# Four of the 64 products by C of each scan run: made by VectorE, not by GpSimd

## The chip, the cores and the metric

The kernel runs on one core of one Trainium2 chip. The metric is the device time of one execution in microseconds (us). The chip's engines each follow a queue of their own: TensorE (PE in the profile, its weight loads PEld), VectorE (DVE), ScalarE (ACT), GpSimd (POOL) and SyncE (SP), which here issues the transfers.

## What is computed

Two sequences of 1024 tokens with 256 features pass through four layers: a linear attention, a state space layer over permuted tokens, a state space layer that runs forward and backward over the tokens, and an attention. The change concerns the state space recurrence of the second and third layers. In the reference (here of the third; the second has the same form):

```python
delta = softplus(einsum('bsr,er->bse', dlt, Wdt) + bdt)
dA = exp(delta[..., None] * A)
dBu = delta[..., None] * Bm[:, :, None, :] * u[..., None]
def step(h, xs):
    dA_t, dBu_t, C_t = xs
    h = dA_t * h + dBu_t
    y = einsum('ben,bn->be', h, C_t)
    return (h, y)
```

There are 512 channels and 16 states for each channel. What the change moves to another engine is part of the product of h by C, inside the `einsum` for y.

## The kernel before

Every engine's program is written out by hand in the order in which it runs, and semaphores join them (`sig`, `wait_ge`, `then_inc`). The recurrence is done in six **runs** (`Run`, q = 0 to 5): two for the second layer, one for each sequence, and four for the third, one for each sequence and direction. Below they are called runs 1 to 6, in the order of their time.

A run is a string of 128 **units**. The sequence of 1024 tokens is cut into two chunks of 512; a unit is one chunk, one of the 16 states and one block (dt) of 128 of the 512 channels. The first chunk's 64 units come first, then the second's. Unit i belongs to step k = i // 4 and to **pair** i // 2, so a run has 64 pairs, each of 128 x 1024 elements, in a ring of five buffers `r.H[pair % HS]` with HS = 5. For unit i:

- ScalarE makes the decay exp(delta A) (`decay`, L931) into one of four buffers. It also scales the operands of u by B (`scale_b`, L908, and `spread_b`, L915) and, in the first chunk, keeps each pair's last column as the start of the second chunk (`keep`, L923, signal `carried`). Its call for pair p stands at i = 2p + 5, behind that unit's decay.
- TensorE forms u = delta x B in one of four PSUM banks (`form_u`, L840 for odd steps, L846 for even ones). It runs three units ahead of the scans, and needs the scan four units back to be done.
- VectorE scans: `tensor_tensor_scan` at L1000, h = a h + u, with a from SBUF and u from PSUM. A new pair's first scan waits until the pair five before it is added up.
- GpSimd multiplies the pair in place by C (`run_p`, L1019), two operands in SBUF. It waits for both scans, in the first chunk for `carried`, and for the row of C, which SyncE loads for each step into one of two buffers (`run_sp`, L801).
- TensorE adds the products up into four PSUM banks (`add_up`, L865); in its order pair p is added at i = 2p + 7. At four places of each chunk it adds a skip product too (`add_skip`, L872).

At unit 71 (`TAKEN_AT`) the first chunk's sum is complete and is taken out of PSUM: by ScalarE (`take_s`, L812) in runs 1, 2, 3 and 5, by VectorE (`take_v`, L818) in runs 4 and 6. After the last unit the second chunk's is taken. In runs 1, 2, 4 and 6 TensorE turns the first chunk's sum back (L1029) between the additions of pairs 62 and 63, and VectorE takes it over with L1036; in runs 3 and 5 TensorE starts the next run's projection (L256) before the additions of pairs 62 and 63.

The lines around the change:

```python
for i in range(UNITS):
    k, dt = divmod(i, 4)
    if i == TAKEN_AT:
        take_y(0)
    w.wait_ge(*decayed.at((q, i)))
    w.wait_ge(*formed.at((q, i)))
    if i >= 2 * HS:
        w.wait_ge(*added.at((q, i // 2 - HS)))
```

Of the kernel before, what the change touches and what calls it, by code (L numbers as in the profile page):

```python
# [8 lines left out]
ALU = mybir.AluOpType  # L9
# [102 lines left out]
def program(nc, T, out):  # L112
    with ExitStack() as ctx:
# [5 lines left out]
        def sig(name, step=1):  # L119
            every.append(Sig(ctx.enter_context(nc.semaphore(name)), step))  # L120
            return every[-1]
# [35 lines left out]
        pe, act, dve, pool = sig("psum_filled"), sig("scalar_done"), sig("vector_done"), sig("pool_done")  # L157
        spread, scaled, formed = sig("b_diagonal"), sig("scaled_by_b"), sig("u_formed")
        decayed, scanned, carried = sig("decayed"), sig("scanned"), sig("carried")
        weighed, added = sig("weighed_by_c"), sig("added_up")  # L160
        taken = sig("y_taken")
        dma = {}

        def transfer(name):
            return dma[name]
# [7 lines left out]
        def area(off, *shape):  # L173
            n = 1
            for s in shape:
                n *= s
            assert off + n <= AW, (off, n)
            v = A[:, off:off + n]
            if len(shape) == 2:
                v = v.rearrange("p (a b) -> p a b", a=shape[0])  # L180
            if len(shape) == 3:
                v = v.rearrange("p (a b c) -> p a b c", a=shape[0], b=shape[1])
            return v
# [429 lines left out]
        CB = [area(WK + 7168 + 512 * j, 512) for j in range(2)]  # L613
        w2all = W2[:, 4992:7040]
        UNITS, PAIRS_N, HS = 128, 64, 5

        class Run:

# [132 lines left out]
        def first_copied(r, j):  # L751
            return (dve if first_state(r, j)[2] else act).at(("dut", r.q, 0, j))
# [31 lines left out]
        def second_half(w, r):  # L784

            w.wait_ge(*act.at(("dut", r.q, 1, 3)))
            w.wait_ge(*dve.at(("dut", r.q, 1, 1)))
# [5 lines left out]
        def run_sp(e, w, r):  # L793
            q = r.q
            w.wait_ge(*transfer(f"c_store{q}").at(0))
            w.wait_ge(*dve.at(("du", q, 0)))
            for k in range(32):
                ci, s = r.steps[k]
                if k >= 2:
                    w.wait_ge(*weighed.at((q, 2 * (k - 2) + 1)))  # L800
                e.dma_start(CB[k % 2], scrc[q][s:s + 1, ci * 512:(ci + 1) * 512].partition_broadcast(128)).then_inc(*transfer(f"c_load{k % 2}").up((q, k)))  # L801

        def took(r, p, j):
# [18 lines left out]
        def run_t(e, w, r, back=None, early=None):  # L822
            q = r.q
            opened = set()

            def form_u(i):
                k, dt = divmod(i, 4)
                if k < 32:
                    ci = r.steps[k][0]
                    if ci == r.order[1]:  # L830
                        second_half(w, r)
                    if i >= 4:
                        w.wait_ge(*scanned.at((q, i - 4)))
                    else:
                        w.wait_ge(*first_copied(r, i))
                    o = PS[:, 4 + i % 4, :]
                    if k % 2:
                        w.wait_ge(*spread.at((q, k, 3)))
                        for j in range(4):
                            t = e.matmul(o[:, j * 128:(j + 1) * 128], r.DUT[:, 4 * ci + j, dt * 128:(dt + 1) * 128], DB[k // 2 % 2][:, j, :],  # L840
                                         start=True, stop=True)
                    else:
                        for j in range(4):
                            w.wait_ge(*(dve.at(("scaled", q, j)) if k == 0 and first_state(r, j)[2] else scaled.at((q, k, j))))
                        for j in range(4):
                            t = e.transpose(o[:, j * 128:(j + 1) * 128], r.G[(2 * k + j) % 6][:, dt * 128:(dt + 1) * 128], ident[:, :])  # L846
                    t.then_inc(*formed.up((q, i)))

            def open_y(ci, j):

                if (ci, j) in opened:
                    return False
                opened.add((ci, j))
                if ci == r.order[0]:
                    w.wait_ge(*(dve if j < 2 else act).at(("dut", q, 1, j)))
                else:
                    w.wait_ge(*took(r, 0, j))
                return True

            def add_up(pair):  # L860
                ci = r.steps[pair // 2][0]
                w.wait_ge(*weighed.at((q, pair)))
                for dt in (pair % 2 * 2, pair % 2 * 2 + 1):
                    for j in range(4):
                        t = e.matmul(PS[:, j, dt * 128:(dt + 1) * 128], r.H[pair % HS][:, dt % 2, j * 128:(j + 1) * 128], ident[:, :],  # L865
                                     start=open_y(ci, j), stop=True, is_transpose=True, skip_group_check=True)
                t.then_inc(*added.up((q, pair)))

            def add_skip(ci, dt):
                w.wait_ge(*dve.at(("diag", q)))  # L870
                for j in range(4):
                    e.matmul(PS[:, j, dt * 128:(dt + 1) * 128], r.U[:, dt, ci * 512 + j * 128:ci * 512 + (j + 1) * 128], diag[:, dt, :],  # L872
                             start=open_y(ci, j), stop=True, skip_group_check=True)

            for i in range(3):
                form_u(i)
            for i in range(UNITS):
                k, dt = divmod(i, 4)
                ci, s = r.steps[k]
                if dt % 2 and i >= 7:  # L880
                    add_up((i - 7) // 2)
                form_u(i + 3)
                if 1 <= i < 5:
                    turn_du_t(e, w, r, 1, i - 1)
                if dt == 3 and 4 <= s < 8:
                    add_skip(ci, s - 4)
            banks.at, banks.held = 4, [[("last y", q, j)] for j in range(4)] + [[("last u", q, j)] for j in range(4)]
            for pair in range(PAIRS_N - 3, PAIRS_N):
                if pair == PAIRS_N - 1 and back:
                    back(0)  # L890
                add_up(pair)
                if pair == PAIRS_N - 3 and early:
                    early()
            if back:
                back(1)
# [78 lines left out]
        def run_v(e, w, r, y, back=None):  # L974
            q = r.q

            def take_y(p):
                for j in range(4):
                    if not by_scalar(r, p, j):
                        take_v(e, w, r, p, j, y)  # L980

            for i in range(UNITS):
                k, dt = divmod(i, 4)
                ci, s = r.steps[k]
                if i == TAKEN_AT:
                    take_y(0)
                if i in (5, 6):
                    copy_du_v(e, w, r, 1, i - 5)
                if i == 6:
                    w.wait_ge(*pe.at(("dut", q, 1, 3)))  # L990
# [4 lines that stand above are left out]
                init = 0.0  # L995
                if ci == r.order[1]:
                    w.wait_ge(*carried.at((q, 2 * s + dt // 2)))
                    init = CAR[:, 4 * s + dt:4 * s + dt + 1]
                h, a, u = (v[:, ::-1] if r.rev else v for v in (r.H[i // 2 % HS][:, dt % 2, :], A_B[i % 4], PS[:, 4 + i % 4, :]))
                e.tensor_tensor_scan(h, a, u, init, ALU.mult, ALU.add).then_inc(*scanned.up((q, i)))  # L1000
            if back:
                back(0)
            take_y(1)
            if back:
                back(1)
            for j in range(4):
                banks.give(("last y", q, j), took(r, 1, j))
                banks.give(("last u", q, j), scanned.at((q, UNITS - 4 + j)))

        def run_p(e, w, r):  # L1010
            q = r.q
            for pair in range(PAIRS_N):
                k = pair // 2
                w.wait_ge(*scanned.at((q, 2 * pair + 1)))
                if r.steps[k][0] == r.order[0]:
                    w.wait_ge(*carried.at((q, pair)))
                w.wait_ge(*transfer(f"c_load{k % 2}").at((q, k)))
                h = r.H[pair % HS]
                e.tensor_tensor(h, h, CB[k % 2].unsqueeze(1).broadcast_to([128, 2, 512]), ALU.mult).then_inc(*weighed.up((q, pair)))  # L1019
# [955 lines left out]
```

## Time and profile before

| | |
|---|---|
| median of three runs | 1950.43 us (1948.98 to 1952.22) |
| span of the profiled execution | 1947.4 us |
| its own time | not given apart from the span |
| VectorE busy | 1602.8 us, 82% of the span |
| TensorE busy | 1845.8 us, 95% |
| ScalarE busy | 1424.0 us, 73% |
| GpSimd busy | 1049.0 us, 54% |
| mean granted clock of TensorE | 0.978 of full speed |

The span goes from the first to the last instruction of the profiled execution. Shares are averages over stages with different limits; the six runs lie between 205 and 1426 us, and what bounds them is read from their own rows. In a timeline neighbouring instructions of one group are merged: the first number is the start, the second the time that they cover, xN their count, and in brackets stands the idle time of the engine before them with what ended it. Recorded durations of VectorE's and GpSimd's instructions overlap a little, so the pace is a little shorter than the duration.

### The profile page before, as it was taken

What the parts mean: (1) busy time and instruction counts of PE and PEld (TensorE: products, weight loads), DVE (VectorE), ACT (ScalarE), POOL (GpSimd) and SP (SyncE); (2) the same over time, 40 slices, a digit from 0 to 9 for tenths busy, and PEclk for the clock granted to TensorE, in tenths of its full rate; (3) what the DMA queues carried; (4) which work ended last, traced back from release to release, by engine and by line L of the source; (5) the groups of instructions that cost most, each with busy time, mean ns of one, the idle gap of its engine ahead of it and who ended that gap; (6) DMA issues with size and microseconds to landing.
All of it is one profiled execution on the core that took longest, in us unless ns stands there. A gap on an engine that the chain in (4) does not pass through costs nothing.

```text
span 1947.4 us, 32682 instructions
## 1 busy us (share of the span) xinstructions
PE 1845.8 (95%) x12312; PEld 1335.2 (69%) x12312; DVE 1602.8 (82%) x2125; ACT 1424.0 (73%) x2661; POOL 1049.0 (54%) x603
## 2 busy tenths in 40 slices
PE   6989899998999999999999999999998999999997
PEld 3664899848998599969995899689974333332323
DVE  5565799678998699989995999889977999999742
ACT  3426899468993899799974999799954377777775
POOL 3031599526994299939980699479944400003000
PEclk9989899998999999999999999999998799999999
DMA  5022111111111112101110111021101111111000
GB/s 202 1 85 99 61 55 61 44 64 33 56 60 37 52 51 60 51 24 55 56 44 2 44 55 56 24 75 57 56 15 33 37 42 37 37 36 36 18 23 22
DMA packets 57547, 95.18 MB, mean 49 GB/s; under 512 B 14951, under 2 KB 23559, under 8 KB 55982
## 3 DMA queue, kind: packets, MB, share of 16 engines
q1 hardware_dynamic: 55854, 88.90, 14.9%
q0 software_dynamic: 1536, 4.20, 0.7%
q8 instruction: 97, 1.59, 0.3%
q14 instruction: 60, 0.49, 0.1%
HBM read 73.55 MB, written 6.91 MB: 41 GB/s over the span
## 4 chain that ended last, share of the span: by engine, by line
PE 66%; POOL 9%; ACT 9%; DVE 8%; issue 6%; DMA 1%; SPq 1%; DVEq 0%; ACTq 0%; POOLq 0%
PE PS L865 12%; PE PS L840 11%; POOL A L1019 8%; PE PS L256 7%; PE PS L1603 6%; PE PS L1556 6%; PE PS L846 5%; PE PS L1763 5%; PE PS L265 3%; DVE A L1569 2%; PE PS L872 2%; ACT A L931 2%; PE PS L441 2%; ACT A L908 1%; DVE ST L206 1%
## 5 line engine op out<-in xcount | busy, mean ns | idle before, releaser
L1019 POOL TENSOR_TENSOR A<-A 128x1024 f32<-128x1024 f32 x384 | 897.7, 2392 | 228.7 <-ACT small L923 104.4
L931 ACT ACTIVATE A<-A,negA 128x512 f32<-128x512 f32 x768 | 546.7, 714 | 30.8 <-DVE A L1000 24.1
L1000 DVE TENSOR_TENSOR_SCAN A<-A,PS 128x512 f32<-128x512 f32 x384 | 435.8, 1200 | 46.6 <-PE PS L846 24.1
L1000 DVE TENSOR_TENSOR_SCAN A<-A,small,PS 128x512 f32<-128x512 f32 x384 | 453.9, 1258 | 8.0 <-ACT A L931 5.0
L865 PE MATMUL PS<-ident,A 128*128 128x128 f32 x3072 | 409.1, 276 | 21.5 <-ACT A L737 13.1
L840 PE MATMUL PS<-A 128*128 128x128 f32 x3072 | 384.2, 276 | 1.5 <-ACT A L915 1.2
L865 PEld LDWEIGHTS PS<-ident,A 128*128 128x128 f32 x3072 | 352.9, 143 | 31.2 <-ACT A L737 15.6
L840 PEld LDWEIGHTS PS<-A 128*128 128x128 f32 x3072 | 363.2, 192 | 4.3 <-DVE A L1000 2.8
L1569 DVE TENSOR_REDUCE A<-PS 128x1 f32<-128x512 f32 x512 | 319.5, 681 | 40.2 <-PE PS L1556 38.7
L1800 ACT ACTIVATE A<-PS 128x512 f32<-128x512 f32 x512 | 267.4, 602 | 102.1 <-PE PS L1763 101.9
L908 ACT ACTIVATE A<-A,small 128x512 f32<-128x512 f32 x320 | 228.3, 714 | 21.7 <-PE PS L846 21.3
L1556 PE MATMUL PS<-A 99*128 99x512 bf16 x480 | 186.9, 398 | 14.0 <-DMA A<-scr 7.5
L846 PE MATMUL PS<-ident,A 128*128 128x128 f32 x1360 | 190.4, 278 | 5.9 <-ACT A L737 2.6
L256 PE MATMUL PS<-A,W 128*128 128x512 f32 (+1 forms) x416 | 184.9, 598 | 3.3 <-DVE A L766 2.9
L1763 PE MATMUL PS<-A 102*128 102x512 bf16 x480 | 178.4, 385 | 5.1 <-ACT A L1800 4.9
L846 PEld LDWEIGHTS PS<-ident,A 128*128 128x128 f32 x1360 | 158.7, 143 | 11.9 <-issue 4.6
L1534 POOL CAST W<-W 128x32 bf16<-128x32 f32 x32 | 6.8, 211 | 291.7 <-DVE W L1527 216.7
L1556 PEld LDWEIGHTS PS<-A 99*128 99x128 bf16 x480 | 47.1, 98 | 167.1 <-DVE A L1569 122.2
L230 POOL TENSOR_TENSOR RS<-VE,HALF 128x8 f32<-128x8 f32 (+1 forms) x15 | 25.7, 1714 | 245.1 <-DVE VE L225 245.1
L915 ACT ACTIVATE A<-ident,small 128x128 f32<-128x128 f32 x384 | 148.8, 394 | 7.3 <-PE PS L840 7.3
L256 PEld LDWEIGHTS PS<-A,W 128*128 128x128 f32 (+1 forms) x416 | 75.1, 185 | 102.7 <-issue 91.5
L1603 PE MATMUL PS<-A,W 128*32 128x512 f32 x1024 | 135.9, 604 | 0.0
(194 smaller groups left out, 1802.5 us busy)
## 6 DMA issues: line engine op xcount, KB each, us to landing
A<-scrc SPq DMA_DIRECT2D x192, 256.0 KB, 3.1
A<-A SPq DMA_DIRECT2D x360, 32.0 KB
scr<-A SPq DMA_DIRECT2D x4, 1024.0 KB, 4.8
W<-in_wa SPq DMA_DIRECT2D x2, 1536.0 KB, 9.7
X<-in_x SPq DMA_DIRECT2D x4, 512.0 KB, 5.5
scr<-W SPq DMA_DIRECT2D x128, 1.5 KB
out<-X SPq DMA_DIRECT2D x4, 512.0 KB, 2.9
W<-in_w SPq DMA_DIRECT2D x1, 1984.0 KB, 7.7
```

What stands on the lines that cost most here:

```text
L256: t = e.matmul(o[0:M, :], wt(k, m), act_in(k), start=k == 0, stop=k == nk - 1)
L840: t = e.matmul(o[:, j * 128:(j + 1) * 128], r.DUT[:, 4 * ci + j, dt * 128:(dt + 1) * 128], DB[k // 2 % 2][:, j, :], start=True, stop=True)
L846: t = e.transpose(o[:, j * 128:(j + 1) * 128], r.G[(2 * k + j) % 6][:, dt * 128:(dt + 1) * 128], ident[:, :])
L865: t = e.matmul(PS[:, j, dt * 128:(dt + 1) * 128], r.H[pair % HS][:, dt % 2, j * 128:(j + 1) * 128], ident[:, :], start=open_y(ci, j), stop ...
L931: e.activation(A_B[i % 4], r.DT[:, dt, ci * 512:(ci + 1) * 512], ACT.Exp, scale=negA[:, r.n, dt * 16 + s:dt * 16 + s + 1]).then_inc(*decay ...
L1000: e.tensor_tensor_scan(h, a, u, init, ALU.mult, ALU.add).then_inc(*scanned.up((q, i)))
L1019: e.tensor_tensor(h, h, CB[k % 2].unsqueeze(1).broadcast_to([128, 2, 512]), ALU.mult).then_inc(*weighed.up((q, pair)))
L1556: e.matmul(o, SQ[j][0:99, nt * 128:(nt + 1) * 128], SK3[j][0:99, c * 512:(c + 1) * 512], start=True, stop=True).then_inc(*pe.up(("trial", ...
L1569: e.tensor_reduce(NM[:, k % 2, q:q + 1], bank(("trial", k, nt, c)), AX.X, ALU.max, negate=True).then_inc(*dve.up(("trial", k, nt, c)))
L1603: t = e.matmul(PV[32 * j:32 * j + 32, c, :], V[:, tile * 272 + 17 * h:tile * 272 + 17 * h + 32], PX[mt % 2][j][:, c * 512:(c + 1) * 512], ...
L1763: e.matmul(o, SK3[sl][0:102, mt * 128:(mt + 1) * 128], SQ[sl][0:102, c * 512:(c + 1) * 512], start=True, stop=True).then_inc(*pe.up(("scor ...
L1800: e.activation(PX[mt % 2][j][:, c * 512:(c + 1) * 512], bank(key), ACT.Exp).then_inc(*act.up(("weights", u, mt, j, c)))
```

## The change

A table `ON_VECTOR` names pairs 15, 31, 47 and 63. GpSimd leaves them out; VectorE multiplies each of them with one `tensor_tensor`, in place, with the same operands. In VectorE's order pair 15's product stands ahead of the scan of unit 34, pair 31's ahead of unit 66, pair 47's ahead of unit 98, and pair 63's behind the last scan. The product has a signal of its own, and TensorE and the loads of C wait for the one or the other; the loads now wait for both pairs of a step.

```diff
+        ON_VECTOR = (15, 31, 47, 63)
+
+        def weighed_at(q, pair):
+            return (weighed_v if pair in ON_VECTOR else weighed).at((q, pair))
...
                 if k >= 2:
-                    w.wait_ge(*weighed.at((q, 2 * (k - 2) + 1)))
+                    w.wait_ge(*weighed_at(q, 2 * (k - 2)))
+                    w.wait_ge(*weighed_at(q, 2 * (k - 2) + 1))
...
-                w.wait_ge(*weighed.at((q, pair)))
+                w.wait_ge(*weighed_at(q, pair))
...
+            def weigh(pair):
+                k = pair // 2
+                w.wait_ge(*scanned.at((q, 2 * pair + 1)))
+                if r.steps[k][0] == r.order[0]:
+                    w.wait_ge(*carried.at((q, pair)))
+                w.wait_ge(*transfer(f"c_load{k % 2}").at((q, k)))
+                h = r.H[pair % HS]
+                e.tensor_tensor(h, h, CB[k % 2].unsqueeze(1).broadcast_to([128, 2, 512]), ALU.mult).then_inc(*weighed_v.up((q, pair)))
+
             for i in range(UNITS):
                 k, dt = divmod(i, 4)
                 ci, s = r.steps[k]
+                if i % 2 == 0 and i // 2 - 2 in ON_VECTOR:
+                    weigh(i // 2 - 2)
...
+            weigh(PAIRS_N - 1)
             if back:
                 back(0)
             take_y(1)
...
             for pair in range(PAIRS_N):
+                if pair in ON_VECTOR:
+                    continue
```

The order of VectorE's instructions in the first run, of the kernel before. L1000 are the scans (with a carried start from unit 64 on, where `small` is an operand), L1036 and L820 what follows the run:

```order
L1000 SCALAR_TENSOR_TENSOR A<-A,PS 128x512 x5
L748 COPY A<-PS 128x512
L1000 SCALAR_TENSOR_TENSOR A<-A,PS 128x512
L748 COPY A<-PS 128x512
L1000 SCALAR_TENSOR_TENSOR A<-A,PS 128x512 x58
L1000 SCALAR_TENSOR_TENSOR A<-A,small,PS 128x512 x64
L1036 TENSOR_TENSOR A<-PS,A 128x512 x4
L820 COPY A<-PS 128x512 x2
L1036 TENSOR_TENSOR A<-PS,A 128x512 x4
```

And of the changed kernel, in which the scans stand at L1016 and the products at L994, from unit 6 on:

```order
L1016 SCALAR_TENSOR_TENSOR A<-A,PS 128x512 x28
L994 TENSOR_TENSOR A<-A 128x1024
L1016 SCALAR_TENSOR_TENSOR A<-A,PS 128x512 x30
L1016 SCALAR_TENSOR_TENSOR A<-A,small,PS 128x512 x2
L994 TENSOR_TENSOR A<-A 128x1024
L1016 SCALAR_TENSOR_TENSOR A<-A,small,PS 128x512 x32
L994 TENSOR_TENSOR A<-A 128x1024
L1016 SCALAR_TENSOR_TENSOR A<-A,small,PS 128x512 x30
L994 TENSOR_TENSOR A<-A 128x1024
L1055 TENSOR_TENSOR A<-PS,A 128x512 x4
```

The four products stand behind units 33, 65, 97 and 127; everything else keeps its place. On GpSimd the 64 products of a run become 60, and nothing takes their place.

## Rows read from the trace of the kernel before

**Rows 1.** Page, costliest groups: busy, mean ns | idle before, by releaser
```profile
L1019 POOL TENSOR_TENSOR A<-A 128x1024 f32<-128x1024 f32 x384 | 897.7, 2392 | 228.7 <-ACT small L923 104.4
L1000 DVE TENSOR_TENSOR_SCAN A<-A,small,PS 128x512 f32<-128x512 f32 x384 | 453.9, 1258 | 8.0 <-ACT A L931 5.0
```

**Rows 2.** Timeline of DVE, first run, from unit 31 on
```profile
248.32 5.85 DVE L1000 TENSOR_TENSOR_SCAN A<-A,PS 128x512 f32<-128x512 f32 x5 [0.58 <-PE PS L840]
254.46 2.33 DVE L1000 TENSOR_TENSOR_SCAN A<-A,PS 128x512 f32<-128x512 f32 x2 [0.29 <-PE PS L840]
257.12 29.20 DVE L1000 TENSOR_TENSOR_SCAN A<-A,PS 128x512 f32<-128x512 f32 x26 [0.33 <-PE PS L840]
286.24 9.46 DVE L1000 TENSOR_TENSOR_SCAN A<-A,small,PS 128x512 f32<-128x512 f32 x8
296.79 27.11 DVE L1000 TENSOR_TENSOR_SCAN A<-A,small,PS 128x512 f32<-128x512 f32 x23 [1.09 <-ACT A L931]
324.14 8.59 DVE L1000 TENSOR_TENSOR_SCAN A<-A,small,PS 128x512 f32<-128x512 f32 x7 [0.24 <-PE PS L840]
332.94 30.57 DVE L1000 TENSOR_TENSOR_SCAN A<-A,small,PS 128x512 f32<-128x512 f32 x26 [0.21 <-PE PS L840]
365.38 2.48 DVE L1036 TENSOR_TENSOR A<-PS,A 128x512 f32<-128x512 f32 x4 [1.88 <-PE PS L1029]
```

**Rows 3.** Timeline of POOL, first run (pairs 12 to 63), then the third run's last 48
```profile
243.60 9.50 POOL L1019 TENSOR_TENSOR A<-A 128x1024 f32<-128x1024 f32 x4 [1.10 <-DVE A L1000]
254.20 111.89 POOL L1019 TENSOR_TENSOR A<-A 128x1024 f32<-128x1024 f32 x48 [1.10 <-DVE A L1000]
...
716.04 111.91 POOL L1019 TENSOR_TENSOR A<-A 128x1024 f32<-128x1024 f32 x48 [1.09 <-DVE A L1000]
```

**Rows 4.** Who waited for L1019, whole span: us, times
```profile
  PE PS L865: 4.9, 5
```

**Rows 5.** Groups of DVE by form: two operands of 2048 elements
```profile
L774 DVE TENSOR_TENSOR A<-A 128x2048 f32<-128x2048 f32 x12 | 27.5, 2292 | 0.4
```

**Rows 6.** Timeline at 1464 to 1470 us: DVE, then POOL
```profile
1464.62 1.22 DVE L1480 TENSOR_TENSOR A<-A 128x1024 f32<-128x1024 f32 x1
...
1467.74 3.15 DVE L1480 TENSOR_TENSOR A<-A 128x1024 f32<-128x1024 f32 x1
...
1467.31 2.50 POOL L1480 TENSOR_TENSOR A<-A 128x1024 f32<-128x1024 f32 x1 [5.32 <-ACT A L1470]
```

**Rows 7.** Timeline at 1498 us: DVE, then POOL
```profile
1498.22 1.89 DVE L1573 TENSOR_TENSOR W<-A 128x8 f32<-128x8 f32 x1
...
1497.96 2.13 POOL L1484 TENSOR_TENSOR A<-A 128x1024 bf16<-128x1024 f32 x1
1500.05 2.13 POOL L1480 TENSOR_TENSOR A<-A 128x1024 f32<-128x1024 f32 x1
```

**Rows 8.** Timeline of ACT at 250 us: the keep of pair 15
```profile
250.40 0.19 ACT L923 ACTIVATE small<-A 128x2 f32<-128x2 f32 x1
```

**Rows 9.** Timelines at 291 to 296 us: PE, then ACT
```profile
291.23 1.95 PE L840 MATMUL PS<-A 128*128 128x128 f32 x16
293.01 1.04 PE L865 MATMUL PS<-ident,A 128*128 128x128 f32 x8
...
294.09 2.06 ACT L812 ACTIVATE A<-PS 128x512 f32<-128x512 f32 x4 [1.97 <-PE PS L865]
```

**Rows 10.** Timeline of DVE, fourth run, at unit 71
```profile
942.98 2.46 DVE L818 TENSOR_TENSOR A<-A,PS 128x512 f32<-128x512 f32 x4
```

**Rows 11.** Timeline of PE, end of the first run and of the third
```profile
363.82 1.09 PE L865 MATMUL PS<-ident,A 128*128 128x128 f32 x8 [0.85 <-POOL A L1019]
364.75 1.91 PE L1029 MATMUL PS<-ident,A 128*128 128x128 f32 x16
366.49 1.04 PE L865 MATMUL PS<-ident,A 128*128 128x128 f32 x8
...
824.65 3.60 PE L256 MATMUL PS<-A,W 128*96 128x512 f32 x8
828.08 1.91 PE L865 MATMUL PS<-ident,A 128*128 128x128 f32 x16
```

More of the change, by code:

```diff
@@ L159, in program @@
         decayed, scanned, carried = sig("decayed"), sig("scanned"), sig("carried")
-        weighed, added = sig("weighed_by_c"), sig("added_up")
+        weighed, weighed_v, added = sig("weighed_by_c"), sig("weighed_by_c_on_vector"), sig("added_up")
         taken = sig("y_taken")
```

## The prediction

> **What bounds the kernel now.** I read the costliest groups first, then the timelines of the runs, one engine at a time, then the waits. On the page GpSimd's products look like the thing to relieve: 384 of them, 2.39 us each, the largest group of all [rows 1]. The timelines say something else. From pair 16 on GpSimd does 48 products back to back in 111.89 us, 2.33 us each [rows 3]. In the same stretch VectorE scans just as densely: 26 units in 29.20 us in the first chunk, 1.12 us each, and 26 in 30.57 us in the second, 1.18 us each [rows 2], or 2.25 and 2.35 us for a pair. So two engines are full at nearly one pace, and the question is which one holds the other.
>
> The brackets of VectorE's rows answer it. From unit 34 to the last scan it idles 0.29 + 0.33 + 1.09 + 0.24 + 0.21 = 2.16 us, and each time for TensorE's forming of u or for ScalarE's decay, never for a sum that waits for GpSimd [rows 2]. GpSimd falls behind a little in the first chunk: its product of pair 32 starts at 254.20 + 16 x 2.33 = 291.5, while the pair's scans end at 286.24 + 2 x 1.18 = 288.6. That lag of 2.9 us is its largest, and it shrinks in the second chunk, where VectorE is the slower one. The ring of five buffers has room: between the end of a pair's scans and the start of the pair five later lie four pairs, 9.0 us, of which the product and the adding (2.37 + 1.04 us) take 3.4, so that 5.6 us are left for a lag. In the whole trace TensorE waits for GpSimd five times, 4.9 us [rows 4], one of them the 0.85 us at the first run's end [rows 11]. VectorE sets the pace of a run, and work taken off GpSimd frees nothing that anyone waits for, while work put on VectorE is put on the path, except where it falls into an idle stretch.
>
> **The price of one product on VectorE.** Two operands in SBUF, 1024 elements: 1.22 us recorded in a row that ran alone [rows 6]. Instructions overlap by some 0.08 us (a scan is recorded with 1.26 us [rows 1] and goes at 1.18 [rows 2]), so it takes 1.14 us of the queue; half of a product of 2048 elements, 2.29 us, is the same [rows 5]. The same group shows the danger: the next instruction of that kind takes 3.15 us [rows 6]. It starts at 1467.74, GpSimd's product runs from 1467.31 to 1469.81, and 1469.81 + 1.14 is 1470.95, near its end at 1470.89: it stood until GpSimd was done. VectorE's scans have one operand in PSUM, and are not stretched by GpSimd; the moved products have both in SBUF. The Trainium skill, SBUF — State Buffer, "Who interferes with whom", says that a VectorE instruction with two SBUF inputs contends with a GpSimd instruction that reads SBUF, and that issue order decides who is blocked for the other's whole length; this speaks against the change, and the trace agrees [rows 6]. By it each moved product would cost from 1.14 us to 1.14 and a whole GpSimd product.
>
> **Part by part, in run 1.** Pair 15, ahead of unit 34. Its `keep` is done at 250.59 [rows 8], before scan 33 ends (248.32 + 3 x 1.16 = 251.8), so that wait costs nothing. GpSimd's pair 14 ends at about 250.7 and pair 16 starts at 254.20 [rows 3], so nothing is in the way: 1.14 us. Right behind it VectorE idled 0.29 and 0.33 us for TensorE [rows 2], which is late there for reasons of its own (the skip products); 0.62 us is covered, 0.52 remains. The row of C was loaded long before.
>
> Pair 31, ahead of unit 66. Scan 65 now ends at 288.6 + 0.5 = 289.1. GpSimd's pair 30 ends at 254.20 + 15 x 2.33 = 289.2, and its next one, pair 32, is released by the same scan 65. I charge 0.15 us of waiting: 1.3 us. That VectorE gets in between two products of GpSimd is shown once: a tiny product of VectorE, issued at 1498.22 beneath GpSimd's instruction, ends at 1500.11, and GpSimd's next takes its usual 2.13 us [rows 7]. VectorE is now 1.8 us late. What follows is the stall for ScalarE at unit 72, 1.09 us [rows 2]. It comes down from TensorE: the forming of units 70 and 71 (from 291.23), the adding of pair 31 (293.01), ScalarE's four copies (294.09), the decay, the scan [rows 9]. TensorE does not wait for GpSimd here (pair 31 was ready at 291.5), so an earlier product gains nothing. It does need scan 67, which ended at 286.24 + 4 x 1.18 = 291.0, and wanted it at about 292.1, so it has 1.15 us of room. Of the 1.8 us about 1.2 vanish there, and 0.6 remain. The stall exists four times, in runs 1, 2, 3 and 5 (ScalarE's 5.0 us over all second chunks [rows 1]); in runs 4 and 6 VectorE takes the sum itself, without idling [rows 10], and all 1.8 us stay. Both pairs: 4 x 0.6 + 2 x 1.8 = 6.0 us over the six runs.
>
> Pair 47, ahead of unit 98. GpSimd, relieved of pair 31, no longer lags, and is between pairs 46 and 48; VectorE's product stands directly behind scan 97 and is there first. 1.14 us, less the 0.21 us of idling before unit 102 [rows 2]. Behind that 26 scans follow without a gap, so 0.93 us stays: 6 x 0.93 = 5.6 us.
>
> Pair 63, behind the last scan. GpSimd's ended at 254.20 + 111.89 = 366.09 [rows 3], 2.6 us after the last scan (332.94 + 30.57 = 363.51); VectorE's would end about 0.1 + 1.14 = 1.3 us after it, sooner by 1.3. But TensorE adds pair 63 only at 366.49, behind the turning of the first chunk's sum, for which it waits on pair 62 [rows 11]. Pair 62 stays on GpSimd. In the third run the adding begins at 828.08 directly behind the next run's projection [rows 11], with GpSimd done at 827.95 [rows 3]: TensorE again. So the 1.3 us is hidden; VectorE idled 1.88 us there anyway [rows 2]. What is gained is GpSimd's small lag at pair 62, about 0.15 us a run: -0.9 us in all.
>
> GpSimd's 24 products fewer, the new waits on TensorE, and SyncE's wait for both pairs of a step cost nothing: pair 15 used to be ready at about 253.1, as it will be now, and GpSimd runs out of work, not of C.
>
> **Sum.** 6.0 + 5.6 - 0.9 = 10.7 us. Against the profiled span, 1947.4 + 10.7 = 1958.1; the median of the three runs lies 3.0 us above that span, so the forecast is 1950.4 + 10.7 = **1961.1 us**, 0.5% slower. No change can be told from one within 0.2%, 3.9 us.
>
> **Rivals.**
> *GpSimd gets in first.* If at pair 31, where both are due within 0.2 us, GpSimd's next product goes ahead in every run, VectorE stands for 2.33 us more: 6 x 2.33 = 14 us, 1975. How such a block looks stands in [rows 6]; [rows 7] speak against it.
>
> *No cover.* If TensorE and ScalarE are late along with VectorE, none of the idling absorbs anything: three products in six runs, 18 x 1.14 = 20.5 us, 1971. For it: TensorE is dense too, and forms u only after the scan four back. Against it: TensorE's room of 1.15 us. Both together are given one chance.
>
> *Nearly all is hidden.* If TensorE was late at unit 72 by more than I read, so that runs 1, 2, 3 and 5 keep nothing of pairs 15 and 31, and the last product's 1.25 us does count in every run: 2 x 1.8 + 5.6 - 7.5 = +1.7 us, 1952. Against it speak the two ends of runs in [rows 11].
>
> *GpSimd is the pacemaker.* If the ring of five buffers held the scans to GpSimd's pace, each of three products would take 2.33 us off its string and put 1.14 on VectorE, and the end would come 1.25 us sooner: 3 x 1.19 + 1.25 = 4.8 us a run, 29 us, 1921 us. It decides from a lag of some 5.6 us on, and the trace shows 2.9; and VectorE has only 2.16 us of idling to give up from unit 34 on against 3.4 us of new work.
>
> **Chances and range.** My forecast, with sums from 1956 to 1966: 0.58. Slower still by a lost port or no cover: 0.28. Nearly hidden: 0.10. GpSimd the pacemaker: 0.04. The range reaches from 1955, where runs 1, 2, 3 and 5 hide both early products, to 1973, above the case without cover and below the one in which every port is lost. Slower 0.86, within 0.2% 0.10, faster 0.04.
>
> **What would show it.** VectorE should have 24 products with a mean near 1.25 us; one of 3 us or more is a lost port. ScalarE's 5.0 us before the second chunks' scans should be nearly gone, and so the 0.29 and 0.33 us before units 36 and 38. From the first scan to the last, run 1 should be about 1.5 us longer, run 4 some 2.7. The waiting of TensorE for GpSimd should stay about what it is, and the stretch from the last scan to L1036's turn should grow by nothing. I am wrong if the runs become shorter, if the scans' own duration changes, or if VectorE's idling grows by itself behind the products.

## The result and the profile after

The changed kernel takes 1960.91 us (median of four runs, 1957.24 to 1961.37) against 1951.24 us of the kernel before: a ratio of 1.0045, with a 95% interval of 1.0033 to 1.0058. (A ratio given here or below can differ by up to 0.1% from that of the two medians.) It is slower, as forecast, and 1961.1 was close. The trace shows that the sum was nearer than its terms: the number is partly right by luck, since errors of both signs cancel, and one of the rivals that I thought less likely turned out to be a real mechanism.

The page of the changed kernel, its costliest groups for the scans, the products left on GpSimd and ScalarE's decay, columns as in [rows 1]:

```profile
span 1959.0 us, 32684 instructions
...
L1038 POOL TENSOR_TENSOR A<-A 128x1024 f32<-128x1024 f32 x360 | 849.6, 2391 | 270.9 <-DVE A L1016 110.0
L936 ACT ACTIVATE A<-A,negA 128x512 f32<-128x512 f32 x768 | 547.8, 716 | 43.2 <-DVE A L1016 34.0
...
L1016 DVE TENSOR_TENSOR_SCAN A<-A,small,PS 128x512 f32<-128x512 f32 x384 | 454.0, 1255 | 2.9 <-PE PS L845 2.2
```

The span grew from 1947.4 by 11.6 us. GpSimd's products take 48 us less, and what it gained is waiting: 110.0 us of its idle time now ends with a scan of VectorE, where it was 36.4. The scans kept their own 1.26 us, and ScalarE's 5.0 us ahead of them [rows 1] are gone from the list.

The timeline of VectorE in the first run, from unit 31 on, answers to [rows 2]; L994 are the new products:

```profile
250.13 3.63 DVE L1016 TENSOR_TENSOR_SCAN A<-A,PS 128x512 f32<-128x512 f32 x3 [0.58 <-PE PS L845]
253.67 1.20 DVE L994 TENSOR_TENSOR A<-A 128x1024 f32<-128x1024 f32 x1
254.79 33.44 DVE L1016 TENSOR_TENSOR_SCAN A<-A,PS 128x512 f32<-128x512 f32 x30
288.14 2.43 DVE L1016 TENSOR_TENSOR_SCAN A<-A,small,PS 128x512 f32<-128x512 f32 x2
290.48 1.61 DVE L994 TENSOR_TENSOR A<-A 128x1024 f32<-128x1024 f32 x1
292.02 34.36 DVE L1016 TENSOR_TENSOR_SCAN A<-A,small,PS 128x512 f32<-128x512 f32 x29
326.62 3.75 DVE L1016 TENSOR_TENSOR_SCAN A<-A,small,PS 128x512 f32<-128x512 f32 x3 [0.25 <-PE PS L845]
330.29 1.20 DVE L994 TENSOR_TENSOR A<-A 128x1024 f32<-128x1024 f32 x1
331.40 35.24 DVE L1016 TENSOR_TENSOR_SCAN A<-A,small,PS 128x512 f32<-128x512 f32 x30
366.68 1.22 DVE L994 TENSOR_TENSOR A<-A 128x1024 f32<-128x1024 f32 x1
368.37 2.48 DVE L1055 TENSOR_TENSOR A<-PS,A 128x512 f32<-128x512 f32 x4 [0.46 <-PE PS L1048]
```

The 0.29 and 0.33 us before units 36 and 38, the 1.09 us before unit 72 and the 0.21 us before unit 102 have vanished; the products filled them. Pair 31's product took 1.61 us, not 1.20. And GpSimd in the same stretch, answering to [rows 3]:

```profile
256.01 35.00 POOL L1038 TENSOR_TENSOR A<-A 128x1024 f32<-128x1024 f32 x15 [3.57 <-DVE A L1016]
291.99 2.36 POOL L1038 TENSOR_TENSOR A<-A 128x1024 f32<-128x1024 f32 x1 [0.98 <-DMA A<-scrc]
294.54 7.07 POOL L1038 TENSOR_TENSOR A<-A 128x1024 f32<-128x1024 f32 x3 [0.19 <-DVE A L1016]
301.86 25.80 POOL L1038 TENSOR_TENSOR A<-A 128x1024 f32<-128x1024 f32 x11 [0.26 <-DVE A L1016]
330.45 3.26 POOL L1038 TENSOR_TENSOR A<-A 128x1024 f32<-128x1024 f32 x1 [2.79 <-DVE A L1016]
333.93 32.82 POOL L1038 TENSOR_TENSOR A<-A 128x1024 f32<-128x1024 f32 x14 [0.21 <-DVE A L1016]
```

Two things were not in the prediction. GpSimd waits 0.98 us for its row of C ahead of pair 32 (the second row). And pair 48's product is recorded with 3.26 us instead of 2.36, because VectorE's product of pair 47 (330.29) holds the port: the block goes both ways. By "the port" I mean whatever lets only one of the two engines' products of SBUF operands run at a time, as in [rows 6]; the traces show the standing, not the circuit.

To compare kernels I use one piece of each run, **the stretch**: from the start of the merged scans that begin with unit 31 (the row with 0.5 to 0.6 us of idling) to the first instruction behind the run, L1036 in runs 1, 2, 4 and 6 or L820 in runs 3 and 5. In run 1 it is 365.38 - 248.32 = 117.06 us before [rows 2] and 368.37 - 250.13 = 118.24 after. Over the six runs it is 709.7 us before and 721.4 after: +11.7 us, all of the growth of the span. Measured in the traces in the same way:

| stretch, change against before, us | run 1 | 2 | 3 | 4 | 5 | 6 | sum |
|---|---|---|---|---|---|---|---|
| the change | +1.18 | +1.42 | +1.39 | +2.99 | +1.37 | +3.32 | +11.7 |
| only pair 15 | -0.08 | -0.04 | 0.00 | +0.29 | -0.01 | +0.30 | +0.5 |
| only pair 31 | +0.54 | +0.53 | +0.92 | +2.58 | +0.68 | +2.54 | +7.8 |
| only pair 47 | +0.50 | +0.51 | +0.64 | +0.64 | +0.65 | +0.65 | +3.6 |
| only pair 63 | -0.04 | -0.10 | -0.01 | 0.00 | -0.01 | -0.01 | -0.2 |
| products left out | -0.16 | -0.16 | -0.02 | -0.02 | -0.01 | -0.01 | -0.4 |

The four single products add up to the change in the sum of the six runs; run by run they miss it by up to 0.5 us either way. The stretch repeats to about 0.1 us from one trace to the next, while the rest of the span varies by up to 11 us between these traces (1235 to 1246 us outside the stretches); so for parts of a few us it says more than the total times, and each total is given with its interval.

### The profile page after: what moved, and what is told of

The parts are those of the page before. It is cut to its first block, busy times and chain, and to the rows that moved or that the text cites. A ratio compares the mean times of both kernels' runs of the same rounds, so it can differ in the third digit from the quotient of the medians.

```text
span 1959.0 us, 32684 instructions
## 1 busy us (share of the span) xinstructions
PE 1856.5 (95%) x12312; PEld 1340.5 (68%) x12312; DVE 1630.9 (83%) x2149; ACT 1425.4 (73%) x2661; POOL 1002.0 (51%) x579
## 3 DMA queue, kind: packets, MB, share of 16 engines
q8 instruction: 97, 1.59, 0.3%
## 4 chain that ended last, share of the span: by engine, by line
PE 70%; DVE 10%; ACT 9%; POOL 5%; issue 4%; DMA 1%; SPq 1%; DVEq 0%; ACTq 0%; POOLq 0%
PE PS L870 13%; PE PS L845 13%; PE PS L256 8%; PE PS L851 6%; PE PS L1622 6%; PE PS L1575 6%; PE PS L1782 5%; POOL A L1038 5%; PE PS L265 3%; DVE A L1588 2%; PE PS L877 2%; DVE A L1016 2%; ACT A L936 2%; PE PS L441 2%; ACT A L913 1%
## 5 line engine op out<-in xcount | busy, mean ns | idle before, releaser
L1038 POOL TENSOR_TENSOR A<-A 128x1024 f32<-128x1024 f32 x360 | 849.6, 2391 | 270.9 <-DVE A L1016 110.0
L1016 DVE TENSOR_TENSOR_SCAN A<-A,PS 128x512 f32<-128x512 f32 x384 | 434.7, 1199 | 39.2 <-PE PS L851 22.3
L1016 DVE TENSOR_TENSOR_SCAN A<-A,small,PS 128x512 f32<-128x512 f32 x384 | 454.0, 1255 | 2.9 <-PE PS L845 2.2
```

## The experiments

**One product at a time.** Four kernels with the table `ON_VECTOR` cut to one pair; the product behind the last scan stays only for pair 63.

```diff
-        ON_VECTOR = (15, 31, 47, 63)
+        ON_VECTOR = (15,)
...
-            weigh(PAIRS_N - 1)
```

Pair 15. 

> Only pair 15 of each run is made by VectorE, ahead of unit 34. Measure in the trace: the stretch from the start of unit 31's scans to the hand-over behind the run (L1036, or L820 in runs 3 and 5), which was 709.7 us over the six runs before and 721.4 with all four products. Theory (VectorE sets the pace, idling covers): 1.14 us a product, 0.62 covered right behind it, the rest in runs 1, 2, 3 and 5 by the stall at unit 72 (1.09 to 1.30 us); in runs 4 and 6 0.1 to 0.5 us stay. Sum over six runs +0.2 to +1.0 us, the time within 0.1% of before. Rival without cover: 6 x 1.14 = +6.8 us. Rival GpSimd as pacemaker: each run shorter by up to 1.2 us, -7 us.

Measured: 1953.04 us, ratio 1.0013 (1.0000 to 1.0026); the stretch grows by 0.5 us. Each product takes 1.20 us, and in runs 1, 2, 3 and 5 nothing of it is left. The stall at unit 72 shrinks in run 1 from 1.09 us [rows 2] to 1.00, so nearly all the cover had come before it: at unit 38 VectorE is 0.32 us late, where 0.52 was forecast. Neither other theory fits.

Pair 31. 

> Only pair 31 is made by VectorE, ahead of unit 66. With all four its product was recorded with 1.61 to 1.84 us against 1.20 of the others, so it costs 1.6 us of the queue. Theory: alone, it falls into the stall at unit 72 of runs 1, 2, 3 and 5, which leave at most 0.4 us each; runs 4 and 6, where VectorE has no stall, keep 1.2 to 1.6 us each. Sum +2.5 to +4.8 us in the stretch from unit 31 to the hand-over. Rival without cover: 6 x 1.6 = +9.6 us. Rival GpSimd gets in first: a product of 3.5 us. Rival GpSimd as pacemaker: -7 us.

Measured: 1961.10 us, ratio 1.0061 (1.0049 to 1.0073); the stretch grows by 7.8 us, well above the 2.5 to 4.8 expected. The products take 1.71 to 2.00 us, and runs 4 and 6 lose 2.6 us each, more than the product itself. What the rest is comes below, from the granted clock. The whole grew by some 4 us more than the stretch; that part lies outside the runs and is not explained.

Pair 47. 

> Only pair 47 is made by VectorE, ahead of unit 98. Theory: 1.14 us a run, less the 0.21 us of idling before unit 102, nothing else covers: 0.93 us in each of the six runs alike, +5.6 us. GpSimd is not relieved before, and lags by up to 1 us there, so the product may stand for GpSimd's pair 46: up to 1.14 + 0.5 us, +8.5 us in all at most. Rival covered: 0. Rival GpSimd as pacemaker: -7 us.

Measured: 1953.03 us, ratio 1.0015 (1.0005 to 1.0025); the stretch grows by 3.6 us, 0.5 to 0.65 in every run. The product costs the 1.12 us expected and stands for nothing (1.20 us recorded in all six), but more of it is covered. From unit 95 to the end of the last scan it is 40.03 us against 39.37 before, +0.66; beside the 0.21 us before unit 102 some 0.25 us of waits too small to be listed went too, nearly all of them in units 98 to 101. In run 1 TensorE's turning then starts 0.16 us sooner behind the last scan.

Pair 63. 

> Only pair 63, behind the last scan, is made by VectorE. Theory: its sum is ready 1.3 us sooner, but TensorE does not wait for it (turning back or the next projection stands ahead), so nothing comes of it: 0 to -0.15 us a run, 0 to -0.9 us, the time the same as before. Rival (the last product counts): -1.25 us a run, -7.5 us, 0.4% faster than before.

Measured: 1950.83 us, ratio 1.0009 (0.9999 to 1.0018); the stretch changes by -0.2 us. The earlier last product is hidden, as read from [rows 11].

**The products left out.** GpSimd is relieved, and VectorE is not loaded. The four products of each run are not made; TensorE and the loads wait for the pair's scan instead.

```diff
-            return (weighed_v if pair in ON_VECTOR else weighed).at((q, pair))
+            return scanned.at((q, 2 * pair + 1)) if pair in ON_VECTOR else weighed.at((q, pair))
...
-                if i % 2 == 0 and i // 2 - 2 in ON_VECTOR:
-                    weigh(i // 2 - 2)
...
-            weigh(PAIRS_N - 1)
```

> The products by C of pairs 15, 31, 47 and 63 are not made at all (h is added up unweighed there), neither by GpSimd nor by VectorE, so GpSimd is relieved as in the change and VectorE is not loaded. Theory (VectorE sets the pace): the stretch from unit 31 to the hand-over stays at 709.7 us within 1 us, and the time is that of before, 0 to -2 us. Rival GpSimd as pacemaker: three products of 2.33 us fewer in a run and the end 2.5 us sooner, up to -9.5 us a run, -57 us; rival that the last product alone counts: -1.25 us a run or more, -7.5 us or more.

Measured: 1952.11 us, ratio 1.0004 (0.9991 to 1.0017). The timeline of VectorE, first run, from unit 95 on:

```profile
324.32 8.59 DVE L1014 TENSOR_TENSOR_SCAN A<-A,small,PS 128x512 f32<-128x512 f32 x7 [0.24 <-PE PS L845]
333.12 30.57 DVE L1014 TENSOR_TENSOR_SCAN A<-A,small,PS 128x512 f32<-128x512 f32 x26 [0.21 <-PE PS L845]
365.41 2.48 DVE L1052 TENSOR_TENSOR A<-PS,A 128x512 f32<-128x512 f32 x4 [1.72 <-PE PS L1045]
```

The scans and both idle times are those of [rows 2] to 0.01 us; only the idling before the turn went from 1.88 to 1.72 us. Taking 24 products off GpSimd for nothing in return gains 0.4 us. That settles what bounds the runs: even a free version of this change could not have helped.

**One unit later.** The same products, ahead of units 35, 67 and 99.

```diff
-                if i % 2 == 0 and i // 2 - 2 in ON_VECTOR:
+                if i % 2 and i // 2 - 2 in ON_VECTOR:
```

> As the changed kernel, but the products of pairs 15, 31 and 47 stand one unit later in VectorE's order (ahead of units 35, 67 and 99), when GpSimd is already busy with the pair that the scan before released. Same work, same count. Theory (a product with two operands in SBUF stands while GpSimd's runs): at pairs 31 and 47 it waits about 1.2 us more than in the changed kernel and is recorded with 2.3 to 2.9 us; at pair 15 GpSimd's next product waits for ScalarE's keep, so little or nothing changes. 12 x 1.2 = +14 us over the changed kernel, about 1975 us. Rival (no blocking between the two engines): the same time as the changed kernel, 1961, and products of 1.2 us.

Measured: 1963.43 us, ratio 1.0060 (1.0048 to 1.0073); the stretch is 725.9 us, 4.5 above the change, where 14 were expected. In run 1 the timeline of VectorE, then GpSimd's row at the same time:

```profile
293.06 1.20 DVE L994 TENSOR_TENSOR A<-A 128x1024 f32<-128x1024 f32 x1
...
332.45 2.44 DVE L994 TENSOR_TENSOR A<-A 128x1024 f32<-128x1024 f32 x1
...
293.34 10.12 POOL L1038 TENSOR_TENSOR A<-A 128x1024 f32<-128x1024 f32 x4 [0.94 <-DMA A<-scrc]
331.44 2.37 POOL L1038 TENSOR_TENSOR A<-A 128x1024 f32<-128x1024 f32 x1 [2.33 <-DVE A L1016]
```

At pair 47 the theory holds in all six runs: 2.44 us, of which 331.44 + 2.37 - 332.45 = 1.36 us are standing until GpSimd is done. At pair 31 it fails: 1.20 us, since GpSimd was waiting for its row of C and the port was free. I had not asked why GpSimd stands there. The two together give the measured 4.5: pair 47's product costs 1.24 us more in six runs, +7.4, and pair 31's, free to go, 0.5 less, -3.0. That made me look at the load.

**Pair 34, into the stall.** `ON_VECTOR = (34,)`, ahead of unit 72; the product behind the last scan is left out here too.

> Only pair 34 is made by VectorE, ahead of unit 72, that is into the stall for ScalarE (1.09 to 1.30 us in runs 1, 2, 3 and 5; none in runs 4 and 6). Theory: 1.14 us plus a wait for GpSimd's pair 33, which is running there (GpSimd lags 2.9 us): 0.3 to 1 us of standing. In runs 1, 2, 3 and 5 the stall covers 1.1 to 1.3 us, so 0 to 0.9 us stay; in runs 4 and 6 all of 1.4 to 3 us. Sum +3 to +8 us. Without standing for GpSimd: products of 1.2 us, 0 in four runs and 1.14 in two, +2.3 us. Rival without cover: all six runs alike.

Measured: 1967.85 us, ratio 1.0088 (1.0075 to 1.0101), with a quarter of the products the worst so far; the stretch is 726.0 us, +16.3, where +3 to +8 were expected. It is runs 1, 2, 3 and 5, which were to be covered, that lose 3.5 us each; runs 4 and 6 lose 1.1. In run 1, VectorE and then GpSimd from its pair 16 on:

```profile
301.66 3.98 DVE L994 TENSOR_TENSOR A<-A 128x1024 f32<-128x1024 f32 x1
305.57 26.36 DVE L1016 TENSOR_TENSOR_SCAN A<-A,small,PS 128x512 f32<-128x512 f32 x22
...
260.25 44.31 POOL L1037 TENSOR_TENSOR A<-A 128x1024 f32<-128x1024 f32 x19 [1.11 <-DVE A L1016]
308.09 14.23 POOL L1037 TENSOR_TENSOR A<-A 128x1024 f32<-128x1024 f32 x6 [3.52 <-DVE A L1016]
```

The 19 products are pairs 16 to 33 and 35. Pair 33's ends at 260.25 + 18 x 2.33 = 302.2; VectorE has been waiting since 301.66, but pair 35's goes first, without a pause, to 304.56, and only then does VectorE run. So a waiting VectorE does not get in between two products of GpSimd if the second is ready. In [rows 7] it had seemed to, with a product of eight elements; for these sizes that is refuted. The products took 3.98 to 4.21 us in those four runs, and 1.20 in the two where GpSimd had run dry.

The standing is not all that these four runs lose. Less the stall that they fill, 1.09 to 1.30 us, the four products account for 11.3 of 14.0 us. The remaining 0.7 us a run comes with a fall of TensorE's granted clock. In run 1 TensorE first waits 2.12 us for VectorE, until 306.89; then:

```profile
304.00:308.00 4.00, 1.88 (x15) 1.49 (x13) 4.00 (x4) 3.56 (x8) 0.56 (x1) 1.00 0.30 92
308.00:312.00 4.00, 3.99 (x21) 3.94 (x21) 4.00 (x5) 3.80 (x8) 3.91 (x2) 0.57 0.03 8
```

The columns are explained below, under what runs 4 and 6 lose; the 1.00 and 0.57 are the clock. The same fall stands in runs 2, 3 and 5, and not in runs 4 and 6.

Then why did VectorE not stand as long in the changed kernel, where pairs 30 and 32 stand at the same place? There GpSimd's pair 32 was not ready: 0.98 us for its row of C. The row is loaded in 3.1 us into the buffer that pair 29 frees, and used to hide behind two products, 30 and 31; without pair 31 it has one, 2.33 us. Leaving out pair 31 opened the gap; that the loads now wait for both pairs of a step has no part in it here, since GpSimd makes pair 28 before pair 29. A third buffer takes GpSimd's wait away (`k % 2` becomes `k % 3` wherever the rows of C are loaded or read, with a third signal):

```diff
-        AW = 35100
+        AW = 35344
...
-        CB = [area(WK + 7168 + 512 * j, 512) for j in range(2)]
+        CB = [area(WK + 7168 + 512 * j, 512) for j in range(3)]
...
-                if k >= 2:
-                    w.wait_ge(*weighed_at(q, 2 * (k - 2)))
-                    w.wait_ge(*weighed_at(q, 2 * (k - 2) + 1))
+                if k >= 3:
+                    w.wait_ge(*weighed_at(q, 2 * (k - 3)))
+                    w.wait_ge(*weighed_at(q, 2 * (k - 3) + 1))
...
```

> The changed kernel with a third buffer for the rows of C. In the changed kernel GpSimd's pair 32 starts 0.98 us after its pair 30, because it waits for its row of C, whose load was hidden behind two products before and has only one behind which to hide now; VectorE's product of pair 31 got in during that wait (recorded 1.61 to 1.84 us). Theory (GpSimd keeps the port when its next product is ready, as in the kernel with pair 34 alone, whose product took 3.98 to 4.21 us in four runs): with the third buffer pair 32 is ready when pair 30 ends, and pair 31's product on VectorE takes 3.5 to 4.2 us in all six runs; the stretch from unit 31 to the hand-over grows from 721.4 by 8 to 15 us, the time to about 1970 to 1976. Rival (a waiting VectorE gets in between two products of GpSimd, as the prediction had it): products of 1.6 us or less, time as the changed kernel or 1 us less.

Measured: 1981.64 us, ratio 1.0153 (1.0131 to 1.0175). In run 1, VectorE and then GpSimd:

```profile
290.94 3.94 DVE L994 TENSOR_TENSOR A<-A 128x1024 f32<-128x1024 f32 x1
294.81 7.12 DVE L1016 TENSOR_TENSOR_SCAN A<-A,small,PS 128x512 f32<-128x512 f32 x6
303.52 27.10 DVE L1016 TENSOR_TENSOR_SCAN A<-A,small,PS 128x512 f32<-128x512 f32 x23 [1.59 <-ACT A L936]
...
256.46 37.34 POOL L1038 TENSOR_TENSOR A<-A 128x1024 f32<-128x1024 f32 x16 [3.56 <-DVE A L1016]
297.32 7.05 POOL L1038 TENSOR_TENSOR A<-A 128x1024 f32<-128x1024 f32 x3 [3.52 <-DVE A L1016]
```

GpSimd's 16 products, pairs 16 to 30 and 32, now run without a gap to 293.80, and VectorE's, issued at 290.94, comes behind them. All six products of pair 31 take 3.94 to 4.15 us. The stretch is 740.3 us, 18.9 above the change, where 8 to 15 were expected: the mechanism is confirmed, the size was too low. The longer products are 13.9 of it. In runs 1, 2, 3 and 5 a stall at unit 72 comes back behind them, 1.59 us in the third row and 6.5 us in the four runs together. TensorE in run 1:

```profile
296.13 2.95 PE L845 MATMUL PS<-A 128*128 128x128 f32 x16 [2.48 <-DVE A L1016]
298.87 1.91 PE L870 MATMUL PS<-ident,A 128*128 128x128 f32 x8
```

The same matmuls took 1.95 and 1.04 us in the kernel before [rows 9]. TensorE waited 2.48 us for VectorE, and then its granted clock fell to the lower level; with the eight matmuls that follow it lost 2.1 us more by that, which is more than the stall. The clock falls at this place in all six runs.

The control, the kernel before with the same third buffer:

> The kernel before with a third buffer for the rows of C: the control. GpSimd's 48 products already stand back to back there, and VectorE does not wait for them: the stretch stays at 709.7 us within 0.5, the time that of before.

Measured: 1951.48 us, ratio 1.0005 (0.9995 to 1.0016), the stretch 709.6 us. The buffer itself costs and gains nothing.

**What runs 4 and 6 lose.** They lost 3.0 and 3.3 us in the change, the others 1.2 to 1.4. The busy time of the engines and the granted clock (PEclk) in windows around unit 71 of run 4, before and then after; VectorE takes the sum at 942.98 before and at 946.83 after, so the same work lies 3.9 us later in the second:

```profile
942.00:946.00 4.00, 3.12 (x24) 2.35 (x23) 4.00 (x6) 2.33 (x5) 4.00 (x3) 1.00 0.17 40
946.00:950.00 4.00, 4.00 (x35) 3.66 (x34) 4.00 (x4) 3.18 (x6) 4.00 (x3) 1.00 0.17 66
```

```profile
942.00:946.00 4.00, 3.75 (x31) 3.40 (x31) 4.00 (x5) 3.64 (x7) 3.78 (x3) 1.00 0.24 70
946.00:950.00 4.00, 2.22 (x10) 1.34 (x9) 4.00 (x6) 2.18 (x4) 2.18 (x1) 0.84 0.21 68
950.00:954.00 4.00, 4.00 (x29) 4.00 (x28) 4.00 (x5) 3.33 (x6) 3.45 (x2) 0.73 0.01 2
```

Columns: the window, its length, the busy time of PE, PEld, DVE, ACT and POOL with the instructions of each, the clock, the share of DMA, GB/s. VectorE, 1.9 us late within the run, then takes the sum itself for 2.4 us. TensorE stands 1.18 us for it in one piece and has 2.2 us of work in 4, where it had 3.1. Its granted clock, full before, falls to the lower level (0.5 of full speed) for part of two windows, and 10 and then 29 matmuls run where 24 and then 35 did. TensorE comes out late, and VectorE idles more for it: 0.52 us before unit 95 in both runs, where it was 0.17 and 0.25. With pair 31 alone these two runs lost 2.6 us each, of which the product (1.99 us recorded, 1.9 in the queue) explains 1.9; some 0.65 us a run are left for this, about as much as with pair 34. That it is the clock and not the waiting alone is argued from the matmuls' number, not tested. The fall stands near unit 71 of runs 4 and 6 in all four kernels that have pair 31's product on VectorE (the change, pair 31 alone, one unit later, the third buffer) and in none of the nine others. Over all 13 kernels, 78 runs, the clock falls between unit 31 and the last scan 16 times: these eight, and runs 1, 2, 3 and 5 with pair 34 alone and with the third buffer. Before each of the 16 TensorE stood for VectorE, 1.18 to 2.69 us in one piece; in the other 62 its longest wait was shorter. The Trainium skill, TensorE: Matmul & The Clock Gate, "HAM oscillation — how this bites in real kernels", says that gaps in TensorE's work let its clock fall to half in the midst of a kernel. The traces agree on the fall; the page's case is a longer wait, for a transfer.

**Turning first.** At the end of runs 1, 2, 4 and 6 TensorE waits for GpSimd's pair 62 (0.85 us, [rows 11]) with the turning of the first chunk behind it. In the kernel before, the turning was put ahead of pair 62's addition.

```diff
-                if pair == PAIRS_N - 1 and back:
+                if pair == PAIRS_N - 2 and back:
```

> The kernel before (all products on GpSimd), with TensorE turning the first chunk's sum back ahead of the addition of pair 62 instead of behind it, in runs 1, 2, 4 and 6, where it waited 0.7 to 0.85 us for GpSimd's pair 62. Theory: VectorE's L1036 starts 1.5 us sooner, at once behind the last scan, but the second chunk's sum is bound by GpSimd's pair 63 (366.09) and its addition, so 0.4 to 0.6 us a run come out: -1.6 to -2.4 us, about 1949, a little faster than both kernels but near the noise. Rival: 0, or slower if the addition of pair 62 is pushed late by the turning.

Measured: 1953.90 us, ratio 1.0017 (1.0009 to 1.0026), slower. In run 1 the second turn starts 370.74 - 249.96 = 120.78 us behind the start of unit 31's row, where it was 369.70 - 248.32 = 121.38: the 0.6 us were there, as read from the order. They did not reach the end. I blamed a fall of the clock behind run 4 and limited the edit to runs 1 and 2:

```diff
+                if pair == PAIRS_N - (2 if q < 2 else 1) and back:
```

> The kernel before, with TensorE turning the first chunk's sum back ahead of pair 62's addition in runs 1 and 2 only. With all four runs each run came out 0.6 us shorter, but in the fourth TensorE's granted clock, which stood at 1.00 behind the run's end before, fell to 0.57 in the stretch from 1020 to 1024 us, and the whole was not faster. Theory: without runs 4 and 6 that fall does not come, and 2 x 0.6 = 1.2 us are gained, which a measurement of the time can hardly tell: ratio 0.9994, the stretch to the end of L1036's second turn 0.6 us shorter in runs 1 and 2. Rival: slower as with all four, 1.0017.

Measured: 1951.35 us, ratio 1.0003 (0.9992 to 1.0014): no difference. The fall behind run 4 stands in this trace too, although nothing is changed there, so it was not the turning that caused it, and my reason falls. The first version's trace is longer than that of before by 1.0 us between runs 4 and 5 and by 1.4 between runs 5 and 6, but so is that of the limited one, by 1.4 and 1.2, where nothing is changed. Where the 2.4 us of the first version go stays open. No version here beats the kernel before.

## Why the prediction was right, and where it was not

**What bounds the runs: right, and shown.** With the products left out the stretch shortens by 0.4 us of 709.7. GpSimd as pacemaker is refuted, and so is the last product as something anyone waits for.

**The price of one product, 1.14 us: right.** Recorded 1.20, 1.12 us from its start to the next scan's, wherever the port was free. The scans were not stretched or shortened. The prediction had named a mean near 1.25 us and none of 3 us or more; the 24 products have 1.33 and a longest of 1.84.

**Pair 15, 0.52 us left: somewhat high.** Alone it left 0.32 us at unit 38 and 0.3 at the end of runs 4 and 6; in the four others it was covered to nothing, as forecast.

**Pair 31: the step that failed.** I charged 0.15 us of standing and let VectorE in between two products of GpSimd by [rows 7]. The standing was 0.4 to 0.6 us in the change, since GpSimd's pair 30 ran on, and VectorE came next only because the load of C held GpSimd back 0.98 us, which I had called free ("GpSimd runs out of work, not of C"). Without that accident the product takes some 4 us in every run, as the third buffer showed. The rival "GpSimd gets in first", put at 14 us and thought less likely, is what happened in all ten cases in which the next product was ready; it was even too cheap, since the third buffer cost 18.9 us over the change, for the rival left out what TensorE's clock then does. The rule of the Trainium skill that I set beside [rows 6] (SBUF — State Buffer, "Who interferes with whom": issue order decides) spoke against the change, and the runs agree as far as one running product goes. With the next one ready, the measurements go beyond it: GpSimd keeps the port, and VectorE, which issued before that product began, waits for both.

**Both early pairs, 6.0 us over six runs:** measured 0.5 + 7.8 = 8.3 alone. Runs 1, 2, 3 and 5 gave 2.5 together, where 2.4 was forecast. Runs 4 and 6 carry the difference, 2.9 us each instead of 1.8: 0.6 is pair 31's longer standing (1.9 us in the queue instead of 1.3), some 0.65 the fall of TensorE's clock, which no step of mine had, and pair 15 gives 0.2 back.

**Pair 47, 5.6 us:** measured 3.6. The gaps in the rows that I counted as cover (0.21 us) were not all: waits too small to be listed covered as much again.

**Pair 63 and the lag, -0.9 us:** measured -0.2 for the product, and -0.4 for all of GpSimd's relief. The lag at pair 62 is worth 0.16 us in runs 1 and 2 and next to nothing in the four others.

So the 10.7 us had one term 2.3 us too low, one 2.0 us too high, and a gain 0.7 us too large; the three nearly cancel, which is luck, and the 11.7 us of the stretches and the 9.7 us of the medians lie on either side of it. "No cover" is refuted: the 18 products within the runs alone would have cost 18 x 1.12 = 20 us.

## What to carry to other kernels

When two engines are both full at nearly the same pace, look at whose rows have brackets, and for whom they wait: work moved off the engine that nobody waits for gains nothing, and a kernel that leaves that work out altogether shows it in one run. A product with two operands in SBUF on VectorE costs only its own time where GpSimd is not at work; otherwise count on waiting for GpSimd's running product and for the next one too if that is already released, and place it where GpSimd provably idles. A long standing of VectorE can cost more than itself: where TensorE then waits for it, look at the granted clock behind the wait. And a transfer that hides behind two instructions of an engine is part of what changes when one of them is taken away.

## What the hardware showed that I had not expected

- Between VectorE's product and GpSimd's queue the port is not shared in turn. Issued beneath a running product of GpSimd with a further one ready, VectorE's took 3.94 to 4.21 us in ten cases (four with pair 34 alone, six with the third buffer) instead of 1.20; with GpSimd's next one not ready it took 1.6 to 2.4. The small product of [rows 7], which did get in between two, stays unexplained.
- Removing a wait of GpSimd (0.98 us for a row of C, here in run 1) made the changed kernel 20.7 us slower, by closing the gap through which VectorE had got in.
- A delay of 1.9 us on VectorE in front of a step that TensorE needs was enough for the granted clock to fall in a place where it had stood at 1.00. TensorE had waited 1.18 us in one piece. What runs 4 and 6 lost beyond the product itself was some 0.65 us each (pair 31 alone), and 0.7 us in each of four runs with pair 34.
- Outside the six runs the traces of these kernels differ by up to 11 us although their programs are the same there, and the places where the clock falls differ too. Gains below a few us can only be read from a stretch of the trace.
